# Grouped attention on one core: TensorE's step in the order turns, scores, values, job in place of scores, turns, values, job

## What is computed

```python
scores = q @ k.T * scale            # causal: a block of 128 queries sees 1 to 8 blocks of keys
e = exp(scores - max(scores))
p = e / sum(e)
out = p @ v
# L2 alone, in the same loop: q, k of the next group are projected and rotated,
# and the group's output is multiplied by its part of wo and added to acc
```

## Time and profile before

| | |
|---|---|
| median of three runs | 3767.97 us (3765.26 to 3775.6) |
| the profiled execution | 3772.04 us, span on the core 3770.1 us |
| PE busy | 3251.6 us (86%), 16736 matmuls |
| DVE busy | 2463.5 us (65%) |
| ACT busy | 1971.1 us (52%) |
| POOL busy | 1694.2 us (45%) |
| granted TensorE clock, mean | 0.95 |

### The profile page before, as it was taken

The page is one execution under the profiler, slowest core; times in us unless marked ns, Lnnn a source line. Parts: engine busy times, 40 slices in busy tenths (PEclk is TensorE's granted clock), DMA queues, the critical chain, the costliest instruction groups (busy, mean ns, idle before and its releaser), DMA issues. The chain is left out here.

```text
span 3770.1 us, 55139 instructions
## 1 busy us (share of the span) xinstructions
PE 3251.6 (86%) x16736; PEld 2534.8 (67%) x16736; DVE 2463.5 (65%) x4877; ACT 1971.1 (52%) x3957; POOL 1694.2 (45%) x1293
## 2 busy tenths in 40 slices
PE   5788698479898989988995999788889988998988
PEld 4566576148566666666883899656666666886767
DVE  4687554965577878875557565378778885555554
ACT  3787433333376767764333333277667774334333
POOL 1676221742366667752212544377666762221111
PEclk8899899889899999999998999899999999999989
DMA  2000231333201111103320000110111103332132
GB/s 76 24 31 2 77 110 61 130 103 116 62 22 28 30 30 29 27 4 122 110 80 26 1 1 1 35 33 25 26 29 32 30 7 101 109 103 93 64 98 73
DMA packets 81187, 204.07 MB, mean 54 GB/s; under 512 B 17179, under 2 KB 20379, under 8 KB 80662
## 3 DMA queue, kind: packets, MB, share of 16 engines
q1 hardware_dynamic: 80774, 200.74, 17.1%
q10 hardware_dynamic: 144, 0.07, 0.0%
HBM read 170.86 MB, written 4.69 MB: 47 GB/s over the span
## 5 line engine op out<-in xcount | busy, mean ns | idle before, releaser
L1253 POOL TENSOR_TENSOR probs<-probs,row_inverse 128x640 f32<-128x640 f32 (+7 forms) x640 | 738.9, 1159 | 485.5 <-DVE row_inverse L1279 474.3
L541 PE MATMUL psUp<-xnT_part,weights_part 128*128 128x512 f32 x3456 | 834.8, 391 | 3.3 <-DVE hidden L694 2.5
L541 PEld LDWEIGHTS psUp<-xnT_part,weights_part 128*128 128x128 f32 x3456 | 651.6, 189 | 141.6 <-POOL weights_part L515 3.3
L518 POOL TENSOR_TENSOR weights_part<-weights,weights_part 128x768 fp32r<-128x768 f32 x136 | 250.9, 1848 | 1010.9 <-ACT weights_part L597 1010.9
L1267 DVE TENSOR_REDUCE neg_max<-psS 128x1 f32<-128x640 f32 (+7 forms) x640 | 476.7, 745 | 134.4 <-PE psS L1157 133.8
L1220 ACT ACTIVATE probs<-psS,neg_max 128x640 f32<-128x640 f32 (+7 forms) x640 | 475.5, 743 | 142.5 <-DVE neg_max L1267 124.7
L1294 DVE TENSOR_TENSOR probsT_part<-psT,probsT_part 128x512 fp32r<-128x512 f32 (+1 forms) x960 | 501.9, 550 | 62.6 <-ACT probsT_part L1236 54.1
L1236 ACT ACTIVATE probsT_part<-psT 128x512 fp32r<-128x512 f32 (+1 forms) x960 | 440.7, 491 | 162.3 <-PE psT L1169 154.0
L1190 PE MATMUL psO<-probsT_part,v_parts 128*128 128x512 f32 x1440 | 441.4, 422 | 76.8 <-DVE probsT_part L1294 76.4
L1169 PE MATMUL psT<-ident,probs 128*128 128x128 f32 x2880 | 445.2, 278 | 46.5 <-DVE probsT_part L1294 44.5
L551 PE MATMUL psDown<-hidden_part,weights_part 128*128 128x512 f32 x1728 | 446.5, 395 | 32.7 <-DVE hidden_part L714 32.7
(11 more groups left out here) (315 smaller groups left out, 4842.1 us busy)
## 6 DMA issues: line engine op xcount, KB each, us to landing
gates<-gate_rows SPq DMA_DIRECT2D x136, 512.0 KB, 4.0
weights<-in_l_ffn SPq DMA_DIRECT2D x148, 384.0 KB, 4.4
qk_swapped<-qk_raw SPq DMA_DIRECT2D x384, 64.0 KB, 2.0
bc_broadcast<-bc_rows SPq DMA_DIRECT2D x32, 512.0 KB, 4.4
w_group<-in_l_wgroup SPq DMA_DIRECT2D x16, 384.0 KB, 3.2
q_whole<-q_steps SPq DMA_DIRECT2D x32, 128.0 KB
w_o_group<-in_l_wo SPq DMA_DIRECT2D x16, 256.0 KB, 2.8
rope<-in_l_rope SPq DMA_DIRECT2D x2, 1024.0 KB, 5.3
```

The source lines that it names most:

```text
L518: nc.gpsimd.tensor_tensor(w[1][:, j, :], wt[:, j, :], w[0][:, j, :].bitcast(F32), ALU.subtract).then_inc(w_split, 1)
L541: last = nc.tensor.matmul(psU[:, u % 2, g, :], wp[:, j, g * D + k * P:g * D + (k + 1) * P], xp[:, k, cols(half)], start=n == 0, stop=n == ...
L1253: self.nc.gpsimd.tensor_tensor(self.p[:, n % 4, 0:w], self.p[:, n % 4, 0:w], self.rinv[:, at:at + 1].to_broadcast([P, w]), ALU.mult).then_ ...
```

## The change

In TensorE's step the call of `turn` moves ahead of the call of `scores`. Nothing else is edited: the same instructions run, the same semaphores are waited for, with the same counts, and the other engines keep their order.

```diff
         def step(g, s, last):
+            turn(g, s + 4, last)
             scores(g, s + 8, last)
-            turn(g, s + 4, last)
             values(g, s, last)
             self.hooks.pe_step(pe, g, s, last)
```

## The result

| | before | after |
|---|---|---|
| median of four runs each | 3769.25 us | 3904.05 us |
| range of the runs | 3765.26 to 3775.60 | 3902.15 to 3905.53 |
| the profiled execution | 3772.04 us | 3905.53 us |
| granted TensorE clock, mean | 0.950 | 0.948 |

A forecast was written before the change was run, and what follows sets the result against it. PE was taken as the bound, with about a tenth of its time lost to stalls. Sites A to D and the joins summed to 100 us on the profiled 3772.04, giving a median of 3868 us, range 3795 to 3920.

The forecast's parts named there:

- Site A: End of a group (T of 5 blocks in two chunks, S of 4): 35 us in L2, 6 us in L0.
- Site B: Step 7 to 8, T(12) needs its bank at once: 0.9 us, 16 times, 14 us; in L0 7 us.
- joins: S's last mask matmul, now followed by V or a job: 0.05 us over 300 steps, 15 us.
- Site C: Quad of 7 blocks, T(19) waits for unit 18's first bank: 0.35 us, 16 times, 6 us; L0 1 us.
- Site D: Quad of 8 blocks, its steps become a loop: 1.0 us at the next quad's V, 16 times, 16 us; L0 zero.
- one-chunk quads: Quads of 5, 3 and 1 blocks, turned at 4, 3, 2 and 1 blocks: covered as needed, costing nothing.
- What should stay: PE's wait before V for DVE's subtraction: stays near 76 us or shrinks a little.
- Rival 1: PE's waits only move from V to T, leaving at most the joins: 3768 to 3783 us, taken as 3770; chance 0.09.
- Rival 2: Faster: earlier T lets ACT copy earlier, removing DVE's 54.1 us of waiting for copies: 3729 us; chance 0.07.
- Rival 3: Longer stalls also lower the clock, once in each of 20 groups: 54 us more, 3922 us; chance 0.07.

The follow-up runs named there:

- e6: The kernel after, with DVE's subtraction moved ahead of its maximum and ACT's copy ahead of its exponential: 3759.09 us, 0.9971 against the kernel before.

## Why the prediction was right, and where it was mis-sized

Forecast were 3868 us and a range of 3795 to 3920; 3904.05 came. The mechanism held, on the page (the waits above) and under e6, which keeps PE's new order and loses nothing. The sum of 100 us was a quarter too small. The end of a group by the prediction's own steps, with V(24) as zero and the two groups 1285.01 and 1509.78, at which the clock stays at 1.00:

| point in the group's end | before | after | later | predicted |
|---|---|---|---|---|
| T(32), second chunk | 9.36 | 9.55 | 0.19 | 0 |
| job of step 28 | 9.54 | 10.36 | 0.82 | 0.62 |
| V(29) | 11.51 | 13.08 | 1.57 | 1.2 |
| S(38) done | 13.16 | 15.46 | 2.30 | 1.8 |
| T(35), second chunk | 15.92 | 17.88 | 1.96 | 1.4 |
| job of step 31 | 16.19 | 18.60 | 2.41 | 1.9 |
| V(0) | 18.29 | 21.37 | 3.08 | 2.7 |

- **Site A.** Every wait that was named is there, in its order, the last one of 0.46 us before T(36) too (0.7 expected). The failed step is the sentence that T(32)'s wait stays since "DVE's chain starts from the same S(35)". It starts from the same S, but T(31) has moved ahead of it, and the maximum comes 0.2 us later (1517.38, 7.60 behind V(24), against 7.40 in the earlier trace rows). And from the start of a subtraction to T it is 0.82 us (1520.95 to 1521.77), not 0.60 + 0.06. Together that is the 0.37 us by which V(29) was missed, and it stays to the end: 3.1 in place of 2.7. At the loop's turns the end costs 2.8, 1.2, 1.6 and -0.1 us, where 2.0 was taken.
- **Site B.** V(2) to V(8) loses 1.30 us, 0.9 predicted. At V(8) itself it is 0.9, as forecast. Another 0.64 comes at V(4), where the second chunk of T(8) meets a full bank in L2 as well (0.32 us), and 0.3 of that is made good by V(6). I had granted L2 the cover of a job there.
- **The last group.** The prediction counts sites B to D 16 times, as if the last group of each L2 were like the others. It has no projections, and so not the cover that site B reckons with. There V(2) to V(8) loses 4.7 and 5.7 us in place of 0.9. Two of its waits, 1.22 and 0.73 us in the kernel before, are

```profile
1716.46 0.44 PE L1169 MATMUL psT<-ident,probs 128*128 128x128 f32 x2 [2.08 <-DVE probsT_part L1294]
...
1728.36 0.52 PE L1169 MATMUL psT<-ident,probs 128*128 128x128 f32 x3 [2.22 <-DVE probsT_part L1294]
```

  and between them the granted clock is 0.51 over 1717.00 to 1720.00. By the terms of the prediction such a group loses 5 us and its joins; the two lose 24.6 together, some 13 us of the sum's error.
- **Site C.** V(12) to V(16) 0.58, predicted 0.35. **Site D.** V(16) to V(24) 1.40, predicted 1.0; 0.65 of it up to V(21), the first V of the quad behind, so at the entry of the quad of 8 blocks too. The measured values hold the joins of these steps.
- **L0.** 25.6 us where 14 and a share of the joins stood, a third of the sum's error. From V to V, site B is right in L0 (1.86 us a group, 1.65 predicted), and the three ends cost 2.6, 3.5 and 2.6 us (2.05 predicted). The larger parts had no term: 4.5 us up to V(2) of the first group, and 4.5 from V(8) to V(24) of the last one. What makes these two stays open.
- **The one-chunk quads** were put at nothing beyond the joins, and inside them that holds: V(8) to V(12) loses 0.10 us. At T(12), their entry behind the quad of 6 blocks, it doesn't; that was site B.
- **The joins.** In undisturbed one-chunk steps the new order costs 0.03 to 0.07 us a step, with 0.05 taken, so the row nearest had the right size. The Trainium skill's rule ("TensorE: Matmul & The Clock Gate", Step-by-step: what each phase is for) would have had it at zero; the rows say a little more than that. What was left out beside them is that the matmul behind a new wait is recorded longer (0.33 against 0.27 us above): with the joins, PE's busy time grows by 2.4 us an L2 group, and 0.05 a step makes about 1 of them. The values of the table hold this.
- **What should stay.** The prediction let V's wait stay near 76 us; it grew to 101.3. A later subtraction reaches V as it reaches T, and the forecast didn't follow it there.
- **Rival 1**, waits that only change places, is out: both rows grew. **Rival 2**, faster by ACT's copy, did happen in one half: the 54.1 us of DVE's waiting fell to 14.8, but with the maximum in front the time did not follow. The 11 us that e6 gains do not come from it either, as DVE's wait for copies is 111.9 us there.
- **Rival 3**, the clock, holds in part but is a small part of the gap. In four of the eight L2 groups without a loop's turn the time is 88.3 to 88.5 us in place of 87.4 to 87.5, with the clock at 0.98. That is about 1 us a group, not 2.7, and some 4 us in all. The four groups with a turn have 0.94, 0.96, 0.96 and 0.98, against 0.96 each before. The last groups have 0.96 and 0.94, against 1.00 before; counted as rival 3 counts, length times what is missing, that is at most 3.4 and 5.1 us, an estimate. All together it is about a tenth of the gap at most.

Summed up over all groups, from V to V (the joins, 15 us in the prediction, are inside the measured values):

| stretch | L0 predicted | L0 measured | L2 predicted | L2 measured |
|---|---|---|---|---|
| up to V(2) of the first group | no term | 4.5 | no term | 3.6 |
| V(24) to the next V(2), site A | 6 | 8.7 | 35 | 43.0 |
| V(2) to V(8), site B | 7 | 7.4 | 14 | 28.1 |
| V(8) to V(16), site C | 1 | 2.7 | 6 | 12.0 |
| V(16) to V(24), site D | 0 | 3.9 | 16 | 22.1 |
| behind the last V(24) | no term | -1.6 | no term | -1.6 |
| sum | 14 | 25.6 | 71 | 107.1 |

The sites were the right ones and every one of them costs something. The total came as near as it did with each term somewhat too small, and with the last groups and the starts left out; no large errors cancelled.

## What to carry to other kernels

When work is moved in one engine's step, look at the order of the same units on every other engine: an operation moved ahead pays only if its consumers are ahead as well, and T first alone, subtraction first alone, and both copy and subtraction first without T first all lost (3904, 4217 and 4108 us), while the three together gave 3759. To size such a loss, walk one period of the steady loop from row to row, start each wait from what has become of its source, not from where it was, and count the first and the last period by themselves. An experiment that breaks one chain must be searched for the ring that it closes before its result is read as a verdict.

## What the hardware showed that I had not expected

The clock. In the group at 1509.78 the stalls of 1.55, 0.55, 0.43, 1.81 and 0.46 us passed at full clock; in the group at 1330.47, with 1.55, 0.55, 0.43 and 1.81 us at the same places, the clock fell behind the last of them:

```profile
1523.00:1531.20 8.20, 5.50 (x33) 3.74 (x32) 6.50 (x17) 5.25 (x14) 3.34 (x5) 1.00 0.06 12
1343.00:1353.00 10.00, 7.75 (x37) 5.41 (x36) 6.60 (x17) 5.82 (x14) 4.29 (x5) 0.83 0.03 5
```

In the second, right behind the stall of 1.81 us, the matmuls take the time of the lower level, 1.2 GHz: S's 0.49 and 0.40 us are 0.78 and 0.63, and the output job's four matmuls have a pitch of 1.81 us.

```profile
1348.45 0.78 PE L1153 MATMUL psS<-k_part,q_parts 128*128 128x512 f32 x1
1349.03 0.63 PE L1154 MATMUL psS<-k_part,q_parts 128*128 128x512 f32 x1
...
1349.58 2.02 PE L1628 MATMUL psT<-w_o_group,oT 128*128 128x256 f32 x4
1351.39 0.83 PE L1169 MATMUL psT<-ident,probs 128*128 128x128 f32 x4
```

The granted clock over 1348.40 to 1351.40 is 0.51, and 0.98 over 1351.80 to 1353.00. Before, with stalls up to 1.58 us inside them, the eight L2 groups without a turn and the two last ones all kept 1.00. The Trainium skill ("TensorE: Matmul & The Clock Gate", A second HAM failure mode: psum-queue depth-cycling) tells of a clock that goes down and up with short idles at PSUM banks. By this trace that happens here, in four of the eight groups without a turn and in both last ones. What decides between two groups with the same stalls no run of this case shows.
